# Moving VectorE's choice of experts behind the attention's low part, in a fused attention and mixture-of-experts kernel

## The reference, cut to what matters

```python
x = x + xattn(layernorm(x), ctx)      # x: 64 x 64 x 256, ctx: 64 x 64 x 256
x = x + ffn(layernorm(x))

# xattn: 16 heads of 16; 64 context rows per batch, so only the "image" branch has keys
q = rms_norm(linear(x, q_w, q_b), norm_q_w)
k = rms_norm(linear(ctx, k_img_w, k_img_b), norm_k_img_w)
v = linear(ctx, v_img_w, v_img_b)
out = linear(softmax(q @ k.T / 4) @ v, o_w, o_b)

# ffn: 8 experts of inner size 176, the best 2 for each of 4096 rows
topw, sel = top_k(softmax(x @ gate_w.T), 2);  topw = topw / sum(topw)
out = sum over the 2 of topw * ((silu(x @ w1_gate.T) * (x @ w1_up.T)) @ w2.T)
```

## Time and profile before

| | us |
|---|---|
| median of 3 runs (lowest to highest) | 543.46 (541.93 to 543.87) |
| the profiled execution, its own time | 539.4 |
| its span, first to last instruction | 537.6 |
| busy in the span: PE / DVE / ACT / POOL | 435.5 / 413.3 / 320.1 / 303.4 |
| mean granted TensorE clock | 0.927 |
| stage 1: up to SP's first load of a slot | 340.89 |

### The profile page before, as it was taken

The page is one execution under the profiler, slowest core; times in us unless marked ns, Lnnn a source line. Parts: engine busy times, 40 slices in busy tenths (PEclk is TensorE's granted clock), DMA queues, the critical chain, the costliest instruction groups (busy, mean ns, idle before and its releaser), DMA issues.

```text
span 537.6 us, 14646 instructions
## 1 busy us (share of the span) xinstructions
PE 435.5 (81%) x4120; PEld 390.2 (73%) x4120; DVE 413.3 (77%) x1359; ACT 320.1 (60%) x934; POOL 303.4 (56%) x531
## 2 busy tenths in 40 slices
PE   1879899899999999999999861499999999999100
PEld 1668778787877887788878651399999999998000
DVE  7448998999999999999998965176777776766384
ACT  5367778777876787777777620265656666565000
POOL 6634377777777777777776646134445443544200
PEclk9879999999999999999999985599999999999655
DMA  7231442222222222223231114524344343431599
GB/s 225 65 113 43 132 142 75 81 79 80 78 75 82 75 84 74 85 65 89 68 95 53 51 41 129 148 73 131 116 124 130 116 128 119 122 116 60 182 404 351
DMA packets 49559, 60.51 MB, mean 113 GB/s; under 512 B 7615, under 2 KB 43082, under 8 KB 49482
## 3 DMA queue, kind: packets, MB, share of 16 engines
q1 hardware_dynamic: 38026, 38.00, 24.3%
q0 software_dynamic: 6528, 16.86, 9.1%
q10 hardware_dynamic: 4928, 4.72, 2.5%
HBM read 32.86 MB, written 23.27 MB: 104 GB/s over the span
## 4 chain that ended last, share of the span: by engine, by line
PE 68%; DVE 13%; DMA 5%; issue 5%; POOL 3%; SPq 3%; ACT 2%; POOLq 0%; DVEq 0%; ACTq 0%
PE bank L1117 13%; PE bank L1118 11%; PE bank L1119 11%; PE bank L1335 4%; DMA we_l<-expert_out 4%; PE bank L1125 3%; PE bank L1177 3%; PE bank L1231 2%; PE bank L1227 2%; PE bank L1229 2%; PE bank L1228 2%; PE bank L1150 2%; DVE late L835 2%; PE bank L1364 2%; PE bank L1365 2%
## 5 line engine op out<-in xcount | busy, mean ns | idle before, releaser
L527 POOL DMA_INDIRECT expert_out<-probs,late x72 | 70.0, 972 | 93.1 <-ACT probs L720 92.0
L457 POOL DMA_INDIRECT sorted_rows<-row,place_i x64 | 65.9, 1030 | 36.2 <-POOL row L451 25.3
L564 ACT CAST qp_h<-bank 32x256 f16<-32x256 f32 x128 | 46.4, 363 | 31.4 <-PE bank L1150 29.0
L841 DVE TENSOR_TENSOR qp_l<-bank,qp_h 32x256 f16<-32x256 f32 x128 | 52.9, 413 | 4.9 <-ACT qp_h L564 1.9
L1117 PE MATMUL bank<-we_h,xt_h 128*128 x144 | 53.6, 372 | 0.1
L1075 DVE SCALAR_TENSOR_TENSOR probs<-xn,late,bank 128x128 f32<-128x128 f32 x72 | 25.0, 348 | 35.6 <-ACT xn L708 35.6
L708 ACT ACTIVATE xn<-bank 128x176 f32<-128x176 f32 x72 | 22.8, 317 | 42.0 <-PE bank L1119 42.0
L1118 PE MATMUL bank<-we_l,xt_h 128*128 x144 | 47.2, 328 | 0.0
L1119 PE MATMUL bank<-we_h,xt_l 128*128 x144 | 47.1, 327 | 0.0
L1067 DVE TENSOR_TENSOR xt_l<-bank,xt_h 128x256 fp32r<-128x256 f32 x72 | 30.6, 425 | 20.3 <-ACT xt_h L702 16.1
L1335 PE MATMUL bank<-ident,late 128*128 128x128 f32 x144 | 30.7, 296 | 17.4 <-DMA late<-sorted_rows 15.7
(11 more groups left out here) (199 smaller groups left out, 1602.5 us busy)
## 6 DMA issues: line engine op xcount, KB each, us to landing
late<-sorted_rows SPq DMA_DIRECT2D x72, 129.0 KB, 2.1
we_f<-w_exp SPq DMA_DIRECT2D x32, 152.0 KB, 2.4
v_bd<-v_sb SPq DMA_DIRECT2D x128, 34.0 KB, 1.9
ctx_in<-ctx_t SPq DMA_DIRECT2D x32, 128.0 KB, 2.3
we_h<-expert_out SPq DMA_DIRECT2D x8, 512.0 KB, 6.8
we_l<-expert_out SPq DMA_DIRECT2D x8, 512.0 KB, 15.5
x<-x SPq DMA_DIRECT2D x3, 1024.0 KB, 5.8
out<-we_h ACTq DMA_DIRECT2D x8, 256.0 KB, 13.0
```

The source lines that it names most:

```text
L457: pool.indirect_dma_start(sorted_rows, bass.IndirectOffsetOnAxis(ap=place_i[:, t.slot // 2, k, t.par:t.par + 1], axis=0), row[:, k, t.slot ...
L527: pool.indirect_dma_start(expert_out, bass.IndirectOffsetOnAxis(ap=hs[:, r, D:D + 1].bitcast(U32), axis=0), y_sb[:, r % YRING, :], None, b ...
L564: act.copy(q_part(qp_h, t, g), q_bank(g)).then_inc(S["q_h_ready"], 1)
L841: dve.tensor_tensor(q_part(qp_l, t, g), q_bank(g), q_part(qp_h, t, g), ALU.subtract).then_inc(S["q_l_ready"], 1)
```

## The change

In DVE's turn: `neg_max_hi` comes right behind `find_max` (`ln1_stats` stood between them); `ln1_stats` and `ln1_mean` come together behind `q_lo`; `choose` goes from the end of even turns (behind `residual`) to odd turns, behind `att_lo` and ahead of `q_scale`; `route` goes from that place in odd turns to the same place in the even turn after it. PE's `count_rows` follows by one turn, POOL's `send` has lag 7 for 6, so that stage 1 has one turn more, and `tr_x`'s guard against the counts in its bank moves to the other parity. `weights`, `gap_exp`, `ln1` and `qk_rms` stay where they are.

```diff
-LAST = NT + 6
+LAST = NT + 7
...
-            if Tile(j, s - 6).live:
-                send(Tile(j, s - 6))
+            if Tile(j, s - 7).live:
+                send(Tile(j, s - 7))
...
                 find_max(tile(2))
-            if ahead:
-                n = j * SKEW + s + 2 if isinstance(j, int) else None
-                ln1_stats(ahead, {2: x_second, 8: x_third, 9: x_rest}.get(n))
-            if tile(2).live:
                 neg_max_hi(tile(2))
...
                 normalise(tile(3))
-            if ahead:
-                ln1_mean(ahead)
             if tile(1).live:
                 q_lo(tile(1))
+            if ahead:
+                n = j * SKEW + s + 2 if isinstance(j, int) else None
+                ln1_stats(ahead, {2: x_second, 8: x_third, 9: x_rest}.get(n))
+                ln1_mean(ahead)
             if tile(4).live:
                 ln2_norm(tile(4))
             if tile(3).live:
                 att_lo(tile(3))
             if s % 2 == 1 and tile(5).live:
-                route(tile(5), tile(4), (s - 5) // 2 % 2)
+                a = tile(5)
+                a.first = isinstance(j, int) and a.n == 0
+                choose(a, tile(4), (s - 5) // 2 % 2)
+            if s % 2 == 0 and tile(6).live:
+                route(tile(6), tile(5), (s - 6) // 2 % 2)
...
                 residual(tile(3))
-            if s % 2 == 0 and tile(4).live:
-                a = tile(4)
-                a.first = isinstance(j, int) and a.n == 0
-                choose(a, tile(3), (s - 4) // 2 % 2)
...
-            if t.slot % 2 == 0:
+            if t.slot % 2 == 1:
                 need(pe, R["filled_new"], t.pair - 2)
...
-            if s % 2 == 1 and tile(5).live:
-                count_rows(tile(5).pair, (s - 5) // 2 % 2, static and i == 5)
+            if s % 2 == 0 and tile(6).live:
+                count_rows(tile(6).pair, (s - 6) // 2 % 2, static and i == 6)
```

## The result

| | before | changed |
|---|---|---|
| median of 4 runs (lowest to highest), us | 543.66 (541.93 to 543.87) | 595.26 (594.98 to 597.55) |
| the profiled execution, its own time | 539.4 | 594.98 |
| its span | 537.6 | 593.2 |
| mean granted TensorE clock | 0.927 | 0.941 |

The time before has one more run here than where it was given first. The changed kernel takes 1.0966 of it, 95% interval 1.0931 to 1.1001. The direction was forecast, and the chain that sets the turn; but 578 was forecast and the range ended at 590.

What follows compares the result with a forecast made beforehand. PE and DVE were near their limit; the later ln1_mean would delay POOL's qk_rms and ACT's k_scale, giving turns of 10.0 and 10.5 us. Terms +31.3, +1.1, -0.4, +3.3 sum to +35.3: median 578 us, range 562 to 590.

Steps and rivals of the forecast that it cites:

- Rival (a): POOL's wait for the mean is hidden and only DVE's gaps remain: 18.4 us a pair, median 550; chance 0.06.
- rival (c): Granted TensorE clock falls to 1.2 GHz in a stretch: some 6 us more a turn, above the range; chance 0.03.
- parts 1 and 2: DVE's list: choose and route change turns (17.7 us a pair), two regroupings add 0.34 a turn (18.4); both hidden under POOL's wait.
- rival (b): Faster: choose and route's move gains, the regrouping gaps cost nothing; 17.7 us a pair, 539 us, 0.8% faster; chance 0.04.
- part 1: choose and route change turns on DVE: 17.7 us a pair against 18.14, some 6 us gained if nothing else moves.
- `r_qk` by 6.5: POOL's r_qk must be ready by 6.5 us after k_lo for the faster case; the forecast found 7.75.
- The gap between neighbours: On DVE, neg_max_hi needs find_max's result and no longer lies under the stats: 0.13 us of waiting appears.
- up to the `k_lo` of turn 3: Turns 1 and 2 of stage 1, paced by the squares at a low clock: +1.1 us together.
- turns 3 to 30: 14 odd turns of 10.5 us and 13 even of 10.0, less 0.8: 276.2 for 244.93, +31.3 us.
- the end of stage 1: POOL has one send more in front of SP's loads: +3.3 us, bounds nothing and 4.
- `q_hi` follows `tr_q` and `q_lo` follows `q_hi`, so between 0 and 0.2 of it reaches `q_lo`: Odd turn's start: weigh holds tr_q 0.2 us later than k_lo allows; 0.15 taken, making the odd turn 10.5 us.
- with the same distance the median is 578: Last addition: profiled execution forecast at 574.7 us, lying 4.1 under the median as before, so median 578, 6.4% slower.

Runs made afterwards that it cites:

- ln1_back: Changed kernel with ln1_stats and ln1_mean put back at their old places: 539.63 us, 0.9955 of before; 533.93 us, 0.9899, on a chip with prompt signals.
- ln1_only: Kernel before with only the regrouping: neg_max_hi right behind find_max, ln1_stats and ln1_mean behind q_lo: 601.11 us, 1.108 of before.
- qk_first: Changed kernel with qk_rms ahead of ln1 in POOL's list: 561.6 us, 1.0366 of before.
- after_third: Changed kernel, unchanged, run once more on a chip with prompt signals: 576.29 us, 1.0677 of before.
- send_lag7: Kernel before with only POOL's send one turn later (lag 7 for 6) and one turn more: 546.05 us, 1.0066 of before.
- send_first_3: Third run of the changed kernel with send ahead of weights in even turns, on a chip with late signals: 586.34 us, 1.0813 of before.
- send_early: Changed kernel with POOL's send moved behind ctx_lo and ahead of ln1: 578.52 us, 1.0675 of before.
- back_lag6: Changed kernel with ln1_stats and ln1_mean at their old places and send at its old lag of 6: 543.33 us, 1.0023 of before.

## Why the prediction was right and wrong

**Right: what bounds the turn.** The chain is the one written down: mean, POOL's `ln1`, `r_qk`, `k_scale`, exponential, `k_hi`, `k_lo`. `ln1_back` and `ln1_only` show that the loss is the regrouping's, and `qk_first` that it goes through POOL's order. Most signs named in the forecast are there: PE's 1.28 us at `tr_q` shrank to 0.2, PE waits at `tr_k` 1.03 on average (24.8 over 24) where I had 0.9, ACT stands 2.83 in front of `k_scale` where I had over 2, stats to mean is 0.53, and the granted clock was 1.00 in each 50 us from 50 to 350 of the first trace. POOL's wait for the mean is 1.98 us on average where signals are prompt (51.5 over 26), at the upper edge of "about 1 to 2", and 2.65 where they are late. Rival (a) is excluded by that; rival (c), for this kernel, by the clock. Two signs failed where signals are late: the turns (10.18 and 11.98 for 10.0 and 10.5) and SP's first load of a slot (395.37 for 376; 378.33 where they are prompt).

**Right: parts 1 and 2.** Where signals are prompt, `ln1_back` has turns of 9.62 and 8.32 us around 205, and 17.77 a pair from turn 3 to turn 30 (281.84 less 41.90, over 27, doubled); I had 17.7 for part 1 alone. Its gain is 5.4 us (533.93 for 539.38; 2.5 where signals are late, 539.63 for 542.15), as rival (b) has it: the mechanism was real, and the point that I named for it, `r_qk` by 6.5, decided against it in the changed kernel. The gap between neighbours was +0.15 for +0.13, and by itself it costs some 3 us; the rule of the Trainium skill that I weighed (VectorE: DVE Perf Modes, The DRAIN you can't avoid) has no cost there, and the measurement decides against it.

**The sum, term by term** (us against the first trace of before, spans):

| | forecast | signals prompt (`after_third`) | signals late (first trace after) |
|---|---|---|---|
| up to the `k_lo` of turn 3 | +1.1 | +3.0 | +3.1 |
| turns 3 to 30 | +31.3 | +34.6 | +50.7 |
| turns 30, 31 | -0.4 | -1.0 | +0.3 |
| the end of stage 1 | +3.3 | +0.9 | +0.3 |
| stage 2 and the rest | 0 | -0.3 | +1.1 |
| sum | +35.3 | +37.1 | +55.6 |

The start was sized too small: of the +3.0, 0.9 lies ahead of turn 1, and turn 3 took 11.10 us in `after_third` for my 9.7, at a granted clock of 0.57 from 42 to 46 us (10.12 in the first trace after, where it was 1.00). The even turns take 10.09 for my 10.0. The end was sized too large: `send_lag7` shows that the 3.3 us are about right for the kernel before (+3.9), but in the changed one only 0.9 and 0.3 of it appear; that the later `route` covers the rest was not tested. On a chip like the one of the trace that I had, the forecast of 574.7 for the execution's own time stands against 576.47. That it comes so near is in part luck, since the errors have both signs. The last addition of the forecast also has a slip: 574.7 and 4.1 are 578.8, not 578.

**Wrong: two steps.** The first is the step "`q_hi` follows `tr_q` and `q_lo` follows `q_hi`, so between 0 and 0.2 of it reaches `q_lo`". It took the time from the end of a matmul to its reader's start as the 0.03 us or so of the trace. On the chip that the result was measured on it is up to 1.9 us while a send runs, 1.5 reach `q_lo`, and an odd turn takes 12.0, not 10.5. I had looked at POOL's list only for whether it catches up, not for what its DMAs lie against.
The second is the step "with the same distance the median is 578". The profiled execution lay 4.1 us under the median, and 2.5 under the *fastest* of the runs shown (539.4 against 541.93). I took this as a constant to add. The first trace has prompt signals, and no trace shows whether the timed runs beside it had late ones; their times (543.46) are nearest to those of the chips that have. Between the two kinds of chip there is no constant: the medians differ by 3 us in the kernel before, where `q_hi` comes 0.2 later than in the first trace in odd turns (1.47 of `k_lo` for 1.27) and the turn is as long, and by 19 in the changed kernel, where `q_lo` leads to the chain that sets the turn and the second DMA ends at 2.31 of `k_lo` instead of 0.84. In the traces the stretch from the `k_lo` of turn 3 to that of turn 32 has 1.6 of the 3.0 us and 17.5 of the 18.5; what stands behind stage 1 is 1.0 and 1.5 us longer on the chips with late signals, for a reason that was not looked for. The trace of before alone could not have given the 19; the run times could have warned that it was a trace of some other condition, and the range should have been wider upwards.

**Open.** What in the chip holds the signals back, and why three chips do it and two do not. No run took the indirect DMAs away or put plain ones in their place. That they are the cause rests on the odd turns from 9 on, on four placements of the send with which the lateness moved (the changed kernel, `qk_first`, `send_first_3`, `send_early`), and on nothing inside the chip. When in a send a signal is held and when it is let go is open too: the second DMA's end fits most turns, but not SP's in `qk_first` nor `att_hi`'s in `send_early`, which started 0.08 us before that end. What SP waits for at the end of stage 1 in `back_lag6` (first slot load at 342.46 for 339.17 in `ln1_back`) was not found.

## What to carry to other kernels

Before an early step is moved behind other work, ask who waits for it on the slowest list, in front of what: one mean, 2 us later, cost 42 us (576.29 for 533.93, where signals are prompt), since POOL served it ahead of the result that ACT needed in every turn. When the profiled execution lies outside the range of the timed runs, it may show a different condition: repeat it before its numbers carry a sum, and don't add the distance as a constant. And where a chain passes from a matmul to another engine, look at what DMAs POOL issues at that moment.

## What the runs showed of the hardware that was not expected

- On three of five chips, completion signals of matmuls that fell due while POOL issued the two indirect DMAs of a send were in most turns seen only 0.5 to 0.8 us after the second one ended (219.08 to 219.63; 213.58 to 214.32), both waiting engines at one moment. In some places they were seen sooner, at 1.05 us behind the first DMA's end (`qk_first`) or 0.08 ahead of the second's (`send_early`). In the changed kernel PE itself ran on, and DVE's signal to PE was in time (207.28 to 207.43). On two chips the reader was 0.04 to 0.08 us behind the matmul, in the same program.
- Between chips of the two kinds the median differed by 3 us in one order of the instructions (542.1 and 539.4) and by 19 in another (595.26 and 576.29).
- Two DVE neighbours with a result between them start 0.12 to 0.14 us further apart than strangers (1.25 and 1.27 against 1.13 behind the same `find_max`).
